# Layer 2's state loop: the two channel halves joined in one scan, one input product, one output product and one addition per state

## The reference

```python
h = exp(dt * A[:, n]) * h + dt * B[n] * x      # over the 512 positions, h = 0 at the start
y = y + h * C[n]                               # summed over the 16 states
```

## Time and profile before

| | us |
|---|---|
| median of 3 runs | 1637.55 (1633.42 to 1638.33) |
| the profiled execution | 1637.49 |
| its span, first to last instruction | 1635.7 |
| busy: PE / DVE / ACT / POOL | 1261.6 / 1070.3 / 724.0 / 599.8 |
| mean granted TensorE clock | 0.885 of full speed |
| layer 2, four batch rows | about 852 to 1391 us of the span |

### The profile page before, as it was taken

One profiled execution on the slowest core, in us unless ns is written; L12 is line 12 of the kernel. 1 busy time (PEld: TensorE's weight loads), 2 busy tenths in 40 slices (PEclk: granted clock), 3 DMA queues, 4 the chain that ended last, 5 costly groups with the idle time before them and its releaser, 6 DMA issues. The chain is left out here.

```text
span 1635.7 us, 21776 instructions
## 1 busy us (share of the span) xinstructions
PE 1261.6 (77%) x7188; PEld 859.3 (53%) x7188; DVE 1070.3 (65%) x2581; ACT 724.0 (44%) x1526; POOL 599.8 (37%) x597
## 2 busy tenths in 40 slices
PE   1799999998997764666768865976784885888985
PEld 0345564554554653544564652653553554666664
DVE  1266767678786353565556995995997798634444
ACT  0255545544544243333236745653671672343322
POOL 1243344443348533332201441442343244225551
PEclk9999999999999787777787997898797798799998
DMA  8200000000000122430000000000000000001113
GB/s 172 80 1 1 1 1 1 1 1 1 1 6 28 52 78 58 129 116 7 8 1 1 1 0 1 1 0 0 1 0 1 1 1 1 27 14 34 35 34 90
DMA packets 54315, 40.36 MB, mean 25 GB/s; under 512 B 13175, under 2 KB 46685, under 8 KB 54205
## 3 DMA queue, kind: packets, MB, share of 16 engines
q1 hardware_dynamic: 35516, 23.91, 5.0%
q0 software_dynamic: 4544, 9.32, 2.1%
q10 hardware_dynamic: 14146, 5.75, 1.7%
HBM read 25.92 MB, written 13.04 MB: 24 GB/s over the span
## 5 line engine op out<-in xcount | busy, mean ns | idle before, releaser
L762 POOL TENSOR_TENSOR PR<-PR,R 128x256 f32<-128x256 f32 (+3 forms) x128 | 160.9, 1258 | 270.8 <-DVE R L1216 266.0
L1637 POOL TENSOR_TENSOR SA<-SA,H 128x512 f32<-128x512 f32 x64 | 81.6, 1275 | 258.4 <-DVE H L1864 258.4
L1859 DVE TENSOR_TENSOR_SCAN H<-DAS,H 128x512 f32<-128x512 f32 x128 | 174.2, 1399 | 0.0
L415 PEld LDWEIGHTS banks<-we,HH 128*128 128x128 f32 x1024 | 147.3, 214 | 10.3
L415 PE MATMUL banks<-BCR,identR 96*128 96x512 f32 x256 | 110.9, 520 | 53.9 <-DVE H L1864 44.3
L1033 ACT ACTIVATE PR<-banks,NM 128x129 f32<-128x129 f32 (+3 forms) x256 | 132.5, 526 | 43.7 <-DVE NM L1193 42.8
L415 PE MATMUL banks<-we,HH 128*128 128x128 f32 x1024 | 146.4, 297 | 0.0
L415 PEld LDWEIGHTS banks<-PTS,V 128*64 128x64 f32 x1280 | 73.0, 144 | 99.1 <-issue 90.6
L415 PE MATMUL banks<-XNT,we 128*128 128x512 f32 x256 | 120.7, 594 | 0.0
L415 PE MATMUL banks<-PTS,V 128*64 128x128 f32 x1280 | 105.4, 296 | 16.3 <-DVE PTS L1201 9.4
L1201 DVE COPY PTS<-banks 128x128 f32<-128x128 f32 (+3 forms) x128 | 62.2, 486 | 80.9 <-PE banks L903 78.5
(11 more groups left out here) (516 smaller groups left out, 2665.3 us busy)
## 6 DMA issues: line engine op xcount, KB each, us to landing
xsort<-zrow SPq DMA_DIRECT2D x1, 3072.0 KB, 13.1
XS<-xsort SPq DMA_DIRECT2D x12, 256.0 KB, 2.9
ysort<-PTS SPq DMA_DIRECT2D x12, 256.0 KB, 2.2
pj_stage<-in_L_ffn_w_proj SPq DMA_DIRECT2D x1, 2048.0 KB, 9.9
we<-in_L_ffn_we SPq DMA_DIRECT2D x1, 2048.0 KB, 9.6
we<-yrows SPq DMA_DIRECT2D x8, 256.0 KB, 5.0
X<-in_L_attn_resid_pre ACTq DMA_DIRECT2D x4, 256.0 KB, 4.6
xrows<-XN SPq DMA_DIRECT2D x4, 256.0 KB, 2.3
```

The lines of the kernel that those rows point to most:

```text
L415: return nc.tensor.matmul(o, l, r, start=start, stop=stop)
L762: nc.gpsimd.tensor_tensor(p, p, R[:, n, :].unsqueeze(2).to_broadcast([P, 2, w]), ALU.mult).then_inc(pn, 1)
L1637: nc.gpsimd.tensor_tensor(Y[m], Y[m], H[:, n % 2, m, :], ALU.add).then_inc(ya, 1)
L1859: nc.vector.tensor_tensor_scan(H[:, n % 2, m, :], DA[:, n % 4, m, :], H[:, n % 2, m, :], 0.0, ALU.mult, ALU.add).then_inc(scn, 1)
```

## The change

Both halves lie side by side in one run of 1024 positions. The decay of the first position of half 1 is held at zero, so that one scan over 1024 positions starts anew there. Each pair of inputs, scans, products and additions becomes one instruction. The inputs of state n+1 are formed between scan n and product n, and H has three buffers. Y is a tile of its own.

```diff
-                H = sbr("H", [P, 2, 2, S], c=c)
+                H = sbr("H", [P, 3, 2, S], c=c)
+                YY = sbr("YY", [P, 2, S], c=c)
...
-                        for m in range(2):
-                            g.wait_ge(xs, m + 1)
-                            nc.gpsimd.tensor_tensor(Y[m], XM[:, m, :], Dp[:, m:m + 1].to_broadcast([P, S]),
-                                                    ALU.mult).then_inc(ya, 1)
+                        g.wait_ge(xs, 2)
+                        nc.gpsimd.tensor_tensor(Y, XM[:, :, :], Dp[:, :].unsqueeze(2).to_broadcast([P, 2, S]),
+                                                ALU.mult).then_inc(ya, 1)
                         for n in range(NS):
-                            for m in range(2):
-                                g.wait_ge(hc, 2 * n + m + 1)
-                                g.wait_ge(ya, 2 * n + m + 1)
-                                nc.gpsimd.tensor_tensor(Y[m], Y[m], H[:, n % 2, m, :], ALU.add).then_inc(ya, 1)
+                            g.wait_ge(hc, n + 1)
+                            g.wait_ge(ya, n + 1)
+                            nc.gpsimd.tensor_tensor(Y, Y, H[:, n % 3, :, :], ALU.add).then_inc(ya, 1)
...
-                                pe.wait_ge(bm, 2 * n + 2)
+                                pe.wait_ge(bm, n + 1)
                                 rows(n + 1, 0, bp)
...
-                                pe.wait_ge(hc, 2 * n + 2)
+                                pe.wait_ge(hc, n + 1)
                                 rows(n + 1, 1, cp)
...
-                                act.wait_ge(scn, 2 * (n - 3))
+                                act.wait_ge(scn, n - 3)
...
-                                nc.scalar.activation(DA[:, n % 4, m, :], DT[:, m, :], ACT.Exp,
+                                nc.scalar.activation(DA[:, n % 4, m, m:], DT[:, m, m:], ACT.Exp,
...
-                        nc.vector.tensor_tensor(DT[:, :, :], DT[:, :, :], LN, ALU.add).then_inc(dtx, 1)
+                        link(nc.vector.tensor_tensor(DT[:, :, :], DT[:, :, :], LN, ALU.add))
+                        v.wait_ge(dtp, 2)
+                        nc.vector.memset(DA[:, :, 1, 0:1], 0.0).then_inc(dtx, 1)
...
-                        for n in range(NS):
-                            v.wait_ge(bp, n + 1)
-                            for m in range(2):
-                                if n >= 2:
-                                    v.wait_ge(ya, 2 * n + m - 1)
-                                nc.vector.tensor_tensor(H[:, n % 2, m, :], DTX[:, m, :], PS[:, 0, :], ALU.mult).then_inc(bm, 1)
-                            for m in range(2):
-                                v.wait_ge(bm, 2 * n + m + 1)
-                                v.wait_ge(ex, 2 * n + m + 1)
-                                nc.vector.tensor_tensor_scan(H[:, n % 2, m, :], DA[:, n % 4, m, :],
-                                                             H[:, n % 2, m, :], 0.0, ALU.mult, ALU.add).then_inc(scn, 1)
+                        def row_of(k):
+                            return PS[:, k, :].unsqueeze(1).to_broadcast([P, 2, S])
+                        def inputs(n):
+                            v.wait_ge(bp, n + 1)
+                            if n >= 3:
+                                v.wait_ge(ya, n - 1)
+                            nc.vector.tensor_tensor(H[:, n % 3, :, :], DTX[:, :, :], row_of(0), ALU.mult).then_inc(bm, 1)
+                        def scan(n):
+                            h = H[:, n % 3, :, :].rearrange("p m s -> p (m s)")
+                            v.wait_ge(bm, n + 1)
+                            v.wait_ge(ex, 2 * n + 2)
+                            nc.vector.tensor_tensor_scan(h, DA[:, n % 4, :, :].rearrange("p m s -> p (m s)"), h, 0.0,
+                                                         ALU.mult, ALU.add).then_inc(scn, 1)
+                        inputs(0)
+                        for n in range(NS):
+                            scan(n)
+                            if n + 1 < NS:
+                                inputs(n + 1)
                             v.wait_ge(cp, n + 1)
-                            for m in range(2):
-                                v.wait_ge(scn, 2 * n + m + 1)
-                                nc.vector.tensor_tensor(H[:, n % 2, m, :], H[:, n % 2, m, :], PS[:, 1, :],
-                                                        ALU.mult).then_inc(hc, 1)
+                            v.wait_ge(scn, n + 1)
+                            nc.vector.tensor_tensor(H[:, n % 3, :, :], H[:, n % 3, :, :], row_of(1), ALU.mult).then_inc(hc, 1)
                             if n >= 3 and n % 2:
                                 add_expert((n - 3) // 2)
-                        for m in range(2):
-                            v.wait_ge(ya, 2 * NS + m + 1)
-                            last = nc.vector.tensor_tensor(H[:, 0, m, :], Y[m], ZS[:, m, :], ALU.mult)
-                        last.then_inc(yg, 1)
+                        v.wait_ge(ya, NS + 1)
+                        nc.vector.tensor_tensor(H[:, 0, :, :], Y, ZS[:, :, :], ALU.mult).then_inc(yg, 1)
```

More of the change, by code:

```diff
@@ L1616, in layer2 @@
                 E, LN = DA[:, 0, :, :], DA[:, 1, :, :]
-                Y = [SA[:, :, :].rearrange(flat), H1[:, :]]
+                Y = YY[:, :, :]
                 GS = H1[:, :].rearrange("p (t d) -> p t d", t=T)
```

## The result

The change made the kernel slower: 1668.49 us (1664.18 to 1672.15, 4 runs) against 1636.7 (1633.42 to 1638.33, 4 runs), a ratio of 1.0196 with a 95% interval of 1.0164 to 1.0228. The forecast was 1661, in a range of 1644 to 1676. The direction, the place and nearly every term were as forecast; one term was missing, TensorE's clock inside the loop.

A forecast was written before the change was run, and what follows sets the result against it. VectorE, never idle in the loop over states, was taken as the bound; pairs of 11.36 against 11.03 and a later start made each batch row 5.8 us longer, four 23, so 1637.49 + 23 = 1661, range 1644 to 1676.

The forecast's parts named there:

- VectorE is the bound in the loop: Loop over states: VectorE has no idle time, busy 11.03 of 11.03 us per pair, so its gains or losses reach the end.
- Sizes: Joined instructions in the loop: scan occupies 2.19 us, inputs 1.14, products 1.12 on VectorE; addition takes 2.35 on GpSimd.
- The rival of cheap joined operations: Joined addition 1.90 us, scan 1.68, or both: 1646, 1644 or 1636 us in total; chance 0.11.
- Who comes first: After an even state's product the scan starts before the addition, a gap of 0.15 us; after odd ones the addition does.
- The rival with the addition first: For even states too the addition starts before the scan: pairs of 13.74 us, total 1724; chance 0.07.
- Whichever starts first keeps the other out: VectorE instructions with two SBUF operands and GpSimd additions: the first to start holds the other until it is over.
- A pair of 11.36: Two states in steady state, from even scan to even scan, take 11.36 us against 11.03 in the kernel before.
- The start: First four states of a batch row: VectorE waits for TensorE's rows B(2) and B(3), and scan 4 starts 3.46 us later.
- The end: After scan 14, additions 14 and 15 run late; the multiplication by silu(z) ends at 982.71 against 976.89.
- Rival C: VectorE's instruction count decides, scans not held and B in time: 7.7 us less per row, 1607; chance in full 0.06.
- Rival D: TensorE's clock returns later in the first states: two more microseconds per batch row, 1669 us; chance 0.09.

The follow-up runs named there:

- e5: Changed kernel without GpSimd's sixteen additions to Y per batch row, the sum over the states left out: 1632.49 us, ratio 0.9959.
- e3: Changed kernel with one more wait on GpSimd, so an addition starts only when the next state's scan has ended: 1643.26 us, ratio 1.0007.
- e9_halves_new_order: Changed kernel's new order and three buffers, but inputs, scans, products and additions in halves as in the kernel before: 1700.65 us, ratio 1.0358.
- e8: Changed kernel with GpSimd's additions in halves of 512 again, VectorE's instructions still joined: 1640.22 us, ratio 1.0005.
- e6: Changed kernel where TensorE writes the coming row of B once more, unused, in its pause: 1667.37 us, ratio 1.0173.
- e4_both: Changed kernel with row B(n+2) written before the wait for product n and additions waiting for the next state's scan: 1623.52 us, ratio 0.9886.
- e2: Changed kernel where TensorE writes row B(n+2) before it waits for product n, not after it: 1644.12 us, ratio 1.0013.
- e7: Changed kernel's joined instructions in the order of the kernel before (inputs n, scan n, product n, expert): 1673.70 us, ratio 1.0211.

## Why the prediction was right, and where it was short

- *VectorE is the bound in the loop, and a scan and an addition keep each other out.* Shown: without the additions all 64 scans are at 2.28 to 2.29 (e5), with the additions behind the scans all but the last of the first batch row (e3).
- *Sizes.* Joined scan 2.19 plus start-up: 2.28 measured against 2.25. Joined addition 2.35: 2.35. Inputs 1.14, products 1.12: 1.14 and 1.13. The rival of cheap joined operations falls.
- *Who comes first.* For even n the scan, by 0.16 us; it held the port in each of them. The rival with the addition first falls for this kernel; e9_halves_new_order, with halves, shows what that can cost. "Whichever starts first keeps the other out" was right as far as it went; e8 adds who gets the port at a seam. The rule cited from the Trainium skill, page "SBUF — State Buffer", section "Who interferes with whom", is now shown for the scan as the first one too (the addition of 4.28).
- *A pair of 11.36.* Measured 11.37 with the clock up (e6), 11.6 to 12.1 in the changed kernel. This is the step that failed: I let TensorE deliver B 2.15 us after an even product, as at a clock of 1.00. I had counted TensorE's room but not asked what it does to the clock. The pause before an even product's row is 0.98 in the earlier trace rows and 2.16 after, the clock fell behind it, and from scan 4 to scan 14 the first row lost 58.9 - 55.15 = 3.8 us instead of 1.7. I had priced the clock only for the first states. e6, where the clock stays up, has a layer 7.3 us shorter: 25.4 over the kernel before, beside the 23.3 forecast.
- *The start.* VectorE waited 1.67 for B(2), as forecast (1.7), and 2.27 for B(3) (2.95 forecast): TensorE's clock came back earlier than if all had moved with it (0.92 in the stretch from 896 to 900, against 0.77 before). Scan 4 effectively started 2.8 later than before, not 3.46 (910.09 + 1.35, less 909.78, plus the 1.16 by which this execution reached the layer earlier).
- *The end.* From the effective start of scan 14 to the end of the multiplication by silu(z): 12.9 us, forecast as 12.7, against 12.0 before. The projection behind it took 0.4 longer (3.79 against 3.39), with the granted clock at 0.50 from 984 to 988; over the four batch rows its four projections took 3.1 longer in all.
- *Together, in the first batch row:* start 2.8 for 3.46, loop 3.8 for 1.7, end 1.3 for 0.7: about 7.9 where 5.8 was forecast. So the error in the loop was partly offset by the start, which had been priced too high.
- *Rival C, VectorE's own count decides.* It needed both the port free and B within 3.1 us. e4_both makes both true and gives 10.17 per pair; either alone gives 10.75 and 11.28. The forecast's 16 x 4.45 would be a pair of 9.93; the 0.25 above it is the odd scan that is still held.
- *Rival D, a clock that returns later.* Its 1669 is the measured time, but by coincidence: it put two more microseconds per row at the start, and the start was shorter than forecast. The clock's cost came in the loop.

Open: what decides whether the clock falls. The length of the pause alone does not. In the changed kernel the granted clock of the 4 us that follow was below 1.00 behind ten of the thirteen pauses of 2.15 to 2.18 us in its loops and 1.00 behind three (at 1236.25, for one). It was 1.00 behind all 28 pauses of 1.55 in the loops of e3, and yet below 1.00 behind eight of the ten pauses of 1.48 to 1.50 in those of e2. What e6 shows is that with work put into the pauses the fall was gone in every batch row.

## What to carry to other kernels

Before two instructions become one, look at who runs beside them: a longer instruction on a shared port holds it longer, and two halves let the other engine in at the seam (e8). Halves are no remedy by themselves: where the first half is ready earlier it can get in ahead of the other engine (e9). Price a reorder by what it puts next to what, not by the instructions it saves. When an engine's pause gets longer, ask whether its next rows come at the same clock; it was about 7 of 33 us here. And a wait added to an engine with slack can be the repair: additions that start one scan later cost nothing in the loop and took 26 us off it.

## What the runs showed of the hardware that was not expected

- A scan that waits for the port gets it between two back-to-back GpSimd instructions: the scan 2.56 instead of 3.63, the second GpSimd half 3.26 instead of 1.27 (e8).
- TensorE's granted clock fell from 1.00 to a mean of 0.57 over 4 us within a loop in which TensorE is over 80% busy, after a pause of 2.16 us, and did not when 0.7 us of unused matmuls split such pauses (e6). It fell behind pauses of 1.48 to 1.50 too (e2), and stayed behind pauses of 1.55 (e3).
- A scan of 1024 elements takes 2.28, one of 512 takes 1.19: all but 0.1 of it grows with the length.
- A VectorE instruction that waits for the one ahead of it started 0.04 (a scan after its inputs) to 0.10 us (a product after its scan) after that one's end, and 0.08 before it where it waited for nothing (e7).
